# RWKV-7 layer with an int8 feed-forward on one core: the solve step's product as 64x64 matmuls over pairs of heads

## Chip, cores and metric

One core of one Trainium2 chip runs the whole program. The metric is the device time of one execution in microseconds (us), lower is better. A measurement of this kernel is the median of several runs.

## What is computed

The input x is 2 sequences of 4096 tokens with 512 channels, in float32. The layer norm of x feeds an RWKV-7 time mixing block with 16 heads of 32 channels; its result is added to x, and a second layer norm feeds a linear layer on values rounded to int8, which is added again.

```python
def step(s, inp):
    q_, w_, k_, v_, a_, b_ = inp
    sa = jnp.einsum('bhij,bhj->bhi', s, a_)
    s = s * w_[:, :, None, :] + sa[..., None] * b_[:, :, None, :] + v_[..., None] * k_[:, :, None, :]
    return (s, jnp.einsum('bhij,bhj->bhi', s, q_))
...
y = ((yg - mu) / jnp.sqrt(var + EPS)).reshape(Bx, Tx, C) * ln_w + ln_b
y = y + (rk * v.reshape(Bx, Tx, H, HS)).reshape(Bx, Tx, C)
return y * g @ Wo.T
...
x = x + attn(layernorm(x))
x = x + ffn(layernorm(x))
```

The recurrence runs over 4096 tokens per head with a 32x32 state. The kernel computes it in chunks of 32 tokens: inside a chunk the products `sa` of all tokens are the solution of a triangular system, whose inverse is built by squaring, and the state is carried from chunk to chunk.

## The kernel before

A tile is 64 tokens of both sequences (128 rows), so there are 64 tiles, and a tile has two chunks (`NC = 2`). Channels lie on the 128 partitions in 4 blocks, so a block of 128 partitions holds 4 heads of 32 channels each. A system is one head, one sequence and one chunk; a tile has 64 of them, 32 to a chunk. In a tensor such as `tx` (the inverses, 128 x 16 x 32) each quarter of the partitions holds one head, and the 16 groups are 4 channel blocks x 2 sequences x 2 chunks.

Each of the five engines has a program of its own, written out by hand as a sequence of function calls in its `tile_step`; there is no scheduler, and engines meet by semaphores alone. Three tiles are in work at a time: `mix` for tile i+1 (layer norm and the mixed inputs), `project` for tile i (the large projections), `solve` for tile i-1 (the recurrence), `finish` for tile i-2 (output projection and feed-forward). So the solve stages stand between large matmuls on TensorE, which give the other engines time.

The solve of a tile runs so. TensorE forms the scores of pairs of tokens (`scores`, L1187). `power` (L1209, three times), `half_inverse` (L1217) and `inverse` (L1225) make the inverse, with VectorE adding and transposing between them; VectorE's last addition writes `tx` and raises `v_t` (`inverse` of VectorE). Then, for each of the two chunks c:

- `from_values` (L1237) and `from_state` (L1244) sum right-hand sides, outputs and new state in PSUM; VectorE transposes the right-hand sides into `rhs_sb` (L896, `right_hand_sides`) and raises `v_rhs`
- `solve_step` (L1253) multiplies inverse and right-hand sides, and raises `p_u`
- ScalarE writes the solutions twice into `u2`, scaled by `parity[:, 0]` and by `parity[:, 1]` (`solution`, with `by_parity`), and raises `a_u`. `parity` is 1 on the partitions of the even heads and 0 on the others in its first column, and the other way round in its second, so a pair of heads in `u2` is a block-diagonal 64x64 matrix
- `from_solutions` (L1263) multiplies `u2` by `first` into outputs and new state.

Chunk 0 uses the PSUM tensor `bank_b` and chunk 1 `bank_a`. On TensorE `gate_hidden` (L1070, `xm_rg,w_gate`) stands between `solve_step` and `from_solutions` of chunk 0, and `quantised` (L1282, four transposes) between those of chunk 1.

`from_values`, `from_state`, `from_solutions` and `scores` work on pairs of heads: the stationary operand is 64x64 (the block-diagonal copies `vT2`, `s_old2`, `u2`, `bt2`, `kt2`, made by parity), and there are 16 matmuls to a chunk. `solve_step`, `power`, `half_inverse` and `inverse` work on single heads: 32x32 stationary operands, 32 matmuls to a chunk in `solve_step` and 64 to a tile in each of the others. A float32 matmul is two matmul records and two weight loads in the trace, so `solve_step` of one chunk is x64 there.

`bt2`, `kt2`, `pt` and some more lie in the memory of `w_ffn_int`, the integer weights, which are used up once they are converted. The trace names all of them `w_ffn_int`. `bt2` is written by ScalarE (`removal_pairs`) at the start of a tile's solve and read by `scores_b`, and is not read after that. Activations of ScalarE all have the line L504.

Of the kernel before, what the change touches and what calls it, by code (L numbers as in the profile page):

```python
# [14 lines left out]
CHUNK = 32  # L15
# [14 lines left out]
def count(i, per_tile, k):  # L30

    return i * per_tile + k


def rwkv_ffn_kernel(nc, a, out):
# [3 lines left out]
    NC = TB // CHUNK  # L39
    G = KB * B * NC  # L40
    GS = KB * B
# [5 lines left out]
    with ExitStack() as ctx:  # L47
        def sb(name, shape, dt=F32):
            return ctx.enter_context(nc.sbuf_tensor(name, shape, dt))

        def sem(name):
            return ctx.enter_context(nc.semaphore(name))
# [68 lines left out]
        def in_spare(groups):  # L121
# [7 lines left out]
        vT2 = sb("vT2", [P, G, 2, HS])  # L129
# [9 lines left out]
        pw = sb("pw", [P, G, 2, CHUNK])  # L139
        pt = in_spare(G)  # L140
        te = in_spare(G)
        bt2, kt2 = (in_spare(2 * G).rearrange("p (g h) t -> p g h t", h=2) for _ in range(2))
        tx = sb("tx", [P, G, CHUNK])
        rhs_sb = sb("rhs_sb", [P, GS, HS])
        u2 = sb("u2", [P, GS, 2, HS])
        state = [sb(f"state{n}", [P, GS, HS]) for n in range(2)]
# [46 lines left out]
         v_teT, v_t, v_rhs, v_state, v_rkv) = (  # L193
            sem(f"v_{n}") for n in
            "pl vraw vsum vT qkT rk blT klT pm km e ptT sums te t4 tx teT t rhs state rkv".split())
        a_pw, a_u, a_y, a_g, a_b2, a_k2, a_vT2 = (sem(f"a_{n}") for n in "pw u y g b2 k2 vT2".split())
        g_qk, g_qkf, g_rkv = (sem(f"g_{n}") for n in "qk qkf rkv".split())
        sold = sem("sold")

# [58 lines left out]
        def quad(h):  # L258
            return slice(HS * h, HS * h + HS)
# [242 lines left out]
        def _(act):  # L502
# [99 lines left out]
            def by_parity(out_, in_):  # L602
                run(out_[:, :, 0, :], in_, ACT.Identity, scale=parity[:, 0:1])
                return run(out_[:, :, 1, :], in_, ACT.Identity, scale=parity[:, 1:2])

            def solution(m, c):
                act.wait_ge(p_u, count(m, NC, c + 1))
                by_parity(u2, step_part(c, SOL)).then_inc(a_u, 1)
# [56 lines left out]
            def tile_step(i, mix=True, project=True, solve=True, finish=True):  # L665
                j, m, n = i + 1, i - 1, i - 2
                if solve:
                    removal_pairs(m)
                    key_pairs(m)
                if project:  # L670
                    keys(i)
                if finish:
                    squared_heads(n)
                if project:
                    ma_gate(i)
                    a_gate(i)
                    squares(i)
                    mk_gate(i)
                if solve:
                    power(m, 0)  # L680
                if finish:
                    log_variance(n)
                    inverse_deviation(n)
                if project:
                    decay_gate(i)
                if solve:
                    power(m, 1)
                if finish:
                    head_affine(n)
                if solve:  # L690
                    value_pairs(m)
                if project:
                    log_sigmoid(i)
                if mix:
                    normalised(j)
                if solve:
                    power(m, 2)
                if project:
                    values(i)
                if mix:  # L700
                    front_transposed(j)
                if project:
                    log_squares(i)
                    exp_tables()
                    key_decay(i)
                    exponentials(i)
                if mix:
                    low_rank(j)
                if project:
                    queries(i)  # L710
                if solve:
                    solution(m, 0)
                    output_gate(m)
                if project:
                    gate_hidden(i)
                if solve:
                    solution(m, 1)
                if finish:
                    quantised(n)
                if mix:  # L720
                    hidden(j, 0)
                    hidden(j, 1)
                if solve:
                    outputs(m, 0)
                    outputs(m, 1)
# [337 lines left out]
        def _(pe):  # L1063
            mm = nc.tensor.matmul
# [16 lines left out]
            def systems(groups):  # L1081
                return [(n, g, quad(h)) for n, g in groups for h in range(QH)]
# [3 lines left out]
            def head_pairs(groups):  # L1086
                return [(n, g, two_heads(h)) for n, g in groups for h in range(QH // 2)]

            def step_systems(c):

                return systems([(j, j * NC + c) for j in range(GS)])

            def step_pairs(c):

                return head_pairs([(j, j * NC + c) for j in range(GS)])

            def both(t):
                return t.rearrange("p h t -> p (h t)")
# [148 lines left out]

            def solve_step(m, c):
                bank = step_bank(c)
                pe.wait_ge(v_t, count(m, 1, 1))  # L1250
                pe.wait_ge(v_rhs, count(m, NC, c + 1))
                for j, g, q in step_systems(c):
                    ins = mm(bank[q, 4 * CHUNK * j + 3 * CHUNK:4 * CHUNK * (j + 1)], tx[q, g, :], rhs_sb[q, j, :],  # L1253
                             start=False, stop=True, skip_group_check=True)
                ins.then_inc(p_u, 1)

# [155 lines left out]
```

## Time and profile before

| | |
|---|---|
| runs | 3243.76 us median of 3 (3243.23 to 3243.87) |
| the profiled execution: its own time | 3244.0 us |
| its span, first to last instruction | 3242.2 us |
| TensorE matmul / weight load busy | 3029.1 us (93%) / 2675.6 us (83%) |
| VectorE, ScalarE, GpSimd busy | 2626.5 us (81%), 1974.8 us (61%), 1270.6 us (39%) |
| TensorE instructions | 84224 matmul records and as many weight loads |

"PE" is TensorE's matmuls and "PEld" its weight loads, which have rows of their own; DVE is VectorE, ACT ScalarE, POOL GpSimd. Ends of matmuls are modelled, so the time of a stage is best read from its start to the start of the next.

### The profile page before, as it was taken

The numbers are of one execution on the slowest core, as the hardware profiler recorded it, in microseconds if no ns is written. First come the engines' busy times: TensorE is split into PE (matmuls) and PEld (weight loads), VectorE is DVE, ScalarE is ACT, GpSimd is POOL, SyncE is SP. The second block draws the span as 40 slices with busy tenths as digits, with TensorE's granted clock in tenths as the row PEclk, the third lists the DMA queues.
The fourth block names the chain that finished last, engine by engine and source line by source line (L and its number), as shares of the span: only waits on it lengthen the run. The fifth ranks groups of instructions, "written<-read, shape, count | busy, mean of one in ns | idle before, by whom it ended". The sixth has DMA issues, their size and how long they took to land.

```text
span 3242.2 us, 182735 instructions
## 1 busy us (share of the span) xinstructions
PE 3029.1 (93%) x84224; PEld 2675.6 (83%) x84224; DVE 2626.5 (81%) x5443; ACT 1974.8 (61%) x3519; POOL 1270.6 (39%) x1161
## 2 busy tenths in 40 slices
PE   6999999999999999999999999999999999999996
PEld 5888888888888888888888888888888888888884
DVE  4788888888888888887888888887888878888875
ACT  3575675665665665755656656656567566566563
POOL 4334334334334344343344343443433434433332
PEclk9999999999999999999999999999999999999998
DMA  3000000000000000000000000000000000000000
GB/s 118 10 23 20 17 23 19 18 20 18 22 20 17 23 20 17 23 20 17 22 20 19 20 17 23 20 17 23 20 17 23 20 17 20 20 20 20 16 17 19
DMA packets 39380, 70.47 MB, mean 22 GB/s; under 512 B 9812, under 2 KB 10836, under 8 KB 38616
## 3 DMA queue, kind: packets, MB, share of 16 engines
q1 hardware_dynamic: 38616, 58.77, 6.8%
q8 instruction: 664, 10.88, 1.4%
q14 instruction: 100, 0.82, 0.1%
HBM read 41.97 MB, written 16.78 MB: 18 GB/s over the span
## 4 chain that ended last, share of the span: by engine, by line
PE 92%; issue 3%; ACT 2%; DVE 2%; POOL 0%; POOLq 0%; ACTq 0%; DVEq 0%
PE bank L1070 30%; PE bank_a L1209 12%; PE bank L1273 8%; PE bank_a L1187 4%; PE bank L1077 4%; PE bank_b L1187 4%; PE bank_b L1244 3%; PE bank_b L1237 3%; PE bank_a L1237 3%; PE bank_a L1244 3%; PE bank_a L1217 2%; PE bank_a L1225 2%; PE bank L1123 2%; PE bank_a L1263 2%; PE bank_b L1263 2%
## 5 line engine op out<-in xcount | busy, mean ns | idle before, releaser
L504 ACT ACT_TABLE_LOAD x383 | 491.4, 1283 | 19.1 <-DVE shift L761 12.2
L1070 PE MATMUL bank<-xm_rg,w_r 128*128 128x128 f32 x2048 | 285.4, 282 | 4.3 <-issue 3.5
L504 ACT ACTIVATE u<-bank_a,parity 128x256 f32<-128x256 f32 x128 | 53.7, 471 | 386.7 <-PE bank_a L1253 386.7
L1209 PE MATMUL bank_a<-pw,w_ffn_int 32*32 32x64 f32 x16384 | 264.6, 216 | 22.0 <-issue 17.2
L1273 PE MATMUL bank<-w_o,yc 128*128 128x512 f32 x512 | 268.9, 626 | 11.0 <-DVE yc L744 9.3
L1209 PEld LDWEIGHTS bank_a<-pw,w_ffn_int 32*32 32x32 f32 x16384 | 239.6, 106 | 41.7 <-issue 21.3
L1070 PEld LDWEIGHTS bank<-xm_rg,w_r 128*128 128x128 f32 x2048 | 248.9, 191 | 26.8 <-issue 15.9
L504 ACT ACTIVATE u<-bank_b,parity 128x256 f32<-128x256 f32 x128 | 53.8, 471 | 342.3 <-PE bank_b L1253 342.3
L1070 PEld LDWEIGHTS bank<-xm_k,w_k 128*128 128x128 f32 x2048 | 241.2, 194 | 12.5 <-issue 3.8
L1070 PE MATMUL bank<-xm_v,w_v 128*128 128x128 f32 x2048 | 250.2, 275 | 0.0
L1070 PE MATMUL bank<-xm_k,w_k 128*128 128x128 f32 x2048 | 241.7, 277 | 3.5 <-issue 3.5
L1070 PEld LDWEIGHTS bank<-xm_v,w_v 128*128 128x128 f32 x2048 | 239.3, 192 | 0.3
L870 DVE STREAM_TRANSPOSE w_ffn_int<-bank_a 128x512 f32<-128x512 f32 x192 | 137.3, 715 | 90.9 <-ACT pw L504 90.3
L399 POOL TENSOR_TENSOR yc<-yc,rkv 128x512 f32<-128x512 f32 x64 | 82.0, 1281 | 321.7 <-ACT yc L504 321.7
L396 POOL TENSOR_TENSOR kept<-ga,gma 128x512 f32<-128x512 f32 x64 | 81.5, 1274 | 311.6 <-ACT ga L504 311.6
L396 POOL TENSOR_TENSOR kkp<-kk,pinv 128x512 f32<-128x512 f32 x64 | 75.3, 1177 | 288.8 <-DVE kk L744 288.8
L396 POOL TENSOR_TENSOR kmod<-kraw,pinv 128x512 f32<-128x512 f32 x64 | 77.1, 1205 | 261.1 <-ACT pinv L504 261.1
L744 DVE TENSOR_TENSOR first<-bank_a,mask_b 128x1024 f32<-128x1024 f32 x64 | 78.4, 1225 | 106.7 <-PE bank_a L1187 106.7
L399 POOL TENSOR_TENSOR o_sb<-o_sb,x2b 128x512 f32<-128x512 f32 x64 | 81.5, 1274 | 199.3 <-DVE o_sb L968 199.3
L1209 PE MATMUL bank_a<-first,w_ffn_int 32*32 32x64 f32 x8192 | 135.0, 215 | 18.7 <-issue 17.7
L396 POOL TENSOR_TENSOR qkT<-qkT,faaaa_T 128x512 f32<-128x512 f32 x64 | 81.4, 1272 | 166.2 <-DVE qkT L914 166.2
L399 POOL TENSOR_TENSOR xm_wa<-xm_wa,xT 128x512 f32<-128x512 f32 x64 | 89.5, 1399 | 128.4 <-DVE xm_wa L779 128.4
(204 smaller groups left out, 8540.4 us busy)
## 6 DMA issues: line engine op xcount, KB each, us to landing
xin<-in_x SPq DMA_DIRECT2D x128, 128.0 KB, 2.7
xres<-in_x SPq DMA_DIRECT2D x128, 128.0 KB
out<-o_sb SPq DMA_DIRECT2D x128, 128.0 KB, 2.4
w_ffn_int<-in_weight_q SPq DMA_DIRECT2D x1, 2048.0 KB, 10.8
w_k<-in_Wk SPq DMA_DIRECT2D x1, 1024.0 KB
w_r<-in_Wr SPq DMA_DIRECT2D x1, 1024.0 KB
w_v<-in_Wv SPq DMA_DIRECT2D x1, 1024.0 KB
w_o<-in_Wo SPq DMA_DIRECT2D x1, 1024.0 KB, 14.2
```

Of the source, the lines that this page charges most:

```text
L396: return nc.gpsimd.tensor_tensor(out_, in0, in1, ALU.mult)
L399: return nc.gpsimd.tensor_tensor(out_, in0, in1, ALU.add)
L504: return nc.scalar.activation(out_, in_, func, **kw)
L870: V.transpose(pt, pairs(bank_a)[:, :, 0, :]).then_inc(v_ptT, 1)
L1070: ins = mm(bank[:, o * n:(o + 1) * n], weights[:, k, o * P:(o + 1) * P], x[:, k].rearrange("p b t -> p (b t)"), start=(k == 0), stop=(k == ...
L1077: ins = mm(bank[:, o * TOK:(o + 1) * TOK], weights[:, o * P:(o + 1) * P], hidden[:], start=True, stop=True)
L1187: ins = mm(bank[q, 64 * n:64 * n + 64], both(keys_[q, g]), both(aq[q, g, 0:2]), start=True, stop=True)
L1209: ins = mm(bank_a[q, 64 * n:64 * n + 64], pt[q, g, :], source[q, g, 0:2].rearrange("p j t -> p (j t)"), start=True, stop=True)
L1237: mm(bank[q, 4 * CHUNK * j:4 * CHUNK * j + 3 * CHUNK], both(vT2[q, g]), km[q, g].rearrange("p j t -> p (j t)"), start=(j % 4 == 0), stop=F ...
L1244: ins = mm(bank[q, 4 * CHUNK * j:4 * CHUNK * j + 3 * CHUNK], both(s_old2[q, j]), aq[q, g].rearrange("p j t -> p (j t)"), start=False, stop ...
L1263: ins = mm(bank[q, 4 * CHUNK * j + CHUNK:4 * CHUNK * j + 3 * CHUNK], both(u2[q, j]), first[q, g, 2:4].rearrange("p j t -> p (j t)"), start ...
L1273: ins = mm(fb[0][:], yc[:, k * TOK:(k + 1) * TOK], w_o[:, k, :], start=(k == 0), stop=(k == KB - 1))
```

## The change

`solve_step` uses 64x64 stationary operands over pairs of heads, 16 matmuls to a chunk where there were 32. For that ScalarE copies `tx` twice by parity into `tx2`, once per tile, in a new step `inverse_pairs`; `tx2` is the memory of `bt2`. `solve_step` waits for that copy (`a_tx2`) where it waited for `v_t`. The matmuls of a chunk stand where they stood, with the same moving operand `rhs_sb`, 32 columns, now over 64 partitions.

```diff
+        tx2 = bt2
...
+            def inverse_pairs(m):
+                act.wait_ge(v_t, count(m, 1, 1))
+                by_parity(tx2, tx[:]).then_inc(a_tx2, 1)
+
             def solution(m, c):
...
                 if solve:
+                    inverse_pairs(m)
                     solution(m, 0)
                     output_gate(m)
...
             def solve_step(m, c):
                 bank = step_bank(c)
-                pe.wait_ge(v_t, count(m, 1, 1))
+                pe.wait_ge(a_tx2, count(m, 1, 1))
                 pe.wait_ge(v_rhs, count(m, NC, c + 1))
-                for j, g, q in step_systems(c):
-                    ins = mm(bank[q, 4 * CHUNK * j + 3 * CHUNK:4 * CHUNK * (j + 1)], tx[q, g, :], rhs_sb[q, j, :],
+                for j, g, q in step_pairs(c):
+                    ins = mm(bank[q, 4 * CHUNK * j + 3 * CHUNK:4 * CHUNK * (j + 1)], both(tx2[q, g]), rhs_sb[q, j, :],
                              start=False, stop=True, skip_group_check=True)
                 ins.then_inc(p_u, 1)
```

TensorE's instructions around the two solve steps of a tile in the middle, before (a row here counts matmuls, not records; the shape is the output's, and `w_ffn_int` is `tx2`):

```order
L1244 MATMUL bank_b<-aq,s_old 64x96 x16
L1077 MATMUL bank<-hid_g,w_gate 128x128 x4
L1253 MATMUL bank_b<-rhs_sb,tx 32x32 x32
L1070 MATMUL bank<-xm_rg,w_gate 128x128 x4
L1263 MATMUL bank_b<-first,u 64x64 x16
L1123 MATMUL bank<-lo,w_maa 128x128 x16
L1237 MATMUL bank_a<-km,vT 64x96 x16
L1244 MATMUL bank_a<-aq,s_old 64x96 x16
L1253 MATMUL bank_a<-rhs_sb,tx 32x32 x32
L1282 MATMUL bank<-ident_bf,q_bf 128x128 x4
L1263 MATMUL bank_a<-first,u 64x64 x16
```

The same place in the changed kernel, where line numbers are 2 to 6 higher:

```order
L1246 MATMUL bank_b<-aq,s_old 64x96 x16
L1083 MATMUL bank<-hid_g,w_gate 128x128 x4
L1255 MATMUL bank_b<-rhs_sb,w_ffn_int 64x32 x16
L1076 MATMUL bank<-xm_rg,w_gate 128x128 x4
L1265 MATMUL bank_b<-first,u 64x64 x16
L1125 MATMUL bank<-lo,w_maa 128x128 x16
L1239 MATMUL bank_a<-km,vT 64x96 x16
L1246 MATMUL bank_a<-aq,s_old 64x96 x16
L1255 MATMUL bank_a<-rhs_sb,w_ffn_int 64x32 x16
L1284 MATMUL bank<-ident_bf,q_bf 128x128 x4
L1265 MATMUL bank_a<-first,u 64x64 x16
```

Nothing changes place; each solve step goes from 32 matmuls with a 32x32 output to 16 with a 64x32 output.

ScalarE in the same tile, before:

```order
L504 ACT_TABLE_LOAD
L504 ACTIVATE lo<-bank 128x128
L504 ACTIVATE r_raw<-bank 128x512
L504 ACTIVATE u<-bank_b,parity 128x8x32 x2
L504 ACTIVATE gate<-bank 128x512
```

and in the changed kernel:

```order
L505 ACT_TABLE_LOAD
L505 ACTIVATE lo<-bank 128x128
L505 ACTIVATE r_raw<-bank 128x512
L505 ACTIVATE w_ffn_int<-tx,parity 128x16x32 x2
L505 ACTIVATE u<-bank_b,parity 128x8x32 x2
L505 ACTIVATE gate<-bank 128x512
```

The two copies of `tx` stand between the copy of the queries and the solutions of chunk 0; no table load is added.

## Rows read from the trace of the kernel before

**Rows 1.** The page: TensorE's share, and the chain that ended last, by engine.

```profile
PE 3029.1 (93%) x84224; PEld 2675.6 (83%) x84224; DVE 2626.5 (81%) x5443; ACT 1974.8 (61%) x3519; POOL 1270.6 (39%) x1161
...
PE 92%; issue 3%; ACT 2%; DVE 2%; POOL 0%; POOLq 0%; ACTq 0%; DVEq 0%
```

**Rows 2.** Waits of TensorE, whole span: us in total, times, longest us.

```profile
PE bank_a L1253 <- DVE rhs_sb L896: 41.2, 64, 0.6
PE bank_a L1263 <- ACT u L504: 35.2, 64, 0.9
PE bank_a L1209 <- issue: 34.9, 46, 1.5
...
PE bank_a L1225 <- issue: 12.7, 17, 1.1
PE bank_a L1217 <- issue: 11.7, 16, 1.1
```

**Rows 3.** Timeline of PE, both solve steps of a tile: start us, us, what, xrecords.

```profile
1630.36 0.75 PE L1253 MATMUL bank_b<-rhs_sb,tx 32*32 32x32 f32 x64
1631.04 1.16 PE L1070 MATMUL bank<-xm_rg,w_gate 128*128 128x128 f32 x8
1632.13 1.15 PE L1263 MATMUL bank_b<-first,u 64*64 64x64 f32 x32
1633.21 1.17 PE L1123 MATMUL bank<-lo,w_maa 32*128 32x128 f32 x32
1634.32 1.54 PE L1237 MATMUL bank_a<-km,vT 64*64 64x96 f32 x32
1635.69 1.49 PE L1244 MATMUL bank_a<-aq,s_old 64*64 64x96 f32 x32
1637.82 0.74 PE L1253 MATMUL bank_a<-rhs_sb,tx 32*32 32x32 f32 x64 [0.64 <-DVE rhs_sb L896]
1638.56 0.40 PE L1282 MATMUL bank<-ident_bf,q_bf 128*128 128x128 bf16 x4
1639.50 1.15 PE L1263 MATMUL bank_a<-first,u 64*64 64x64 f32 x32 [0.54 <-ACT u L504]
1640.58 1.16 PE L1070 MATMUL bank<-xm_wa,w_hwa 128*128 128x128 f32 x8
```

**Rows 4.** Timeline of PE, the two last stages of the inverse and their successors.

```profile
1621.53 1.29 PE L1217 MATMUL bank_a<-pw,w_ffn_int 32*32 32x32 f32 x128
1622.75 1.98 PE L1273 MATMUL bank<-w_o,yc 128*128 128x512 f32 x4
...
1625.55 1.26 PE L1225 MATMUL bank_a<-pw,w_ffn_int 32*32 32x16 f32 x128
1626.74 1.12 PE L1273 MATMUL bank<-w_o,yc 128*128 128x512 f32 x2
```

**Rows 5.** Weight loads started in the first 0.15 us of L1253 and of L1263.

```profile
1630.35 0.25 PEld L1253 LDWEIGHTS bank_b<-rhs_sb,tx 32*32 32x32 f32 x20
...
1632.12 0.26 PEld L1263 LDWEIGHTS bank_b<-first,u 64*64 64x64 f32 x6
```

**Rows 6.** Groups of PE by form: busy us, mean ns of one record.

```profile
L1209 PE MATMUL bank_a<-pw,w_ffn_int 32*32 32x64 f32 x16384 | 264.6, 216 | 22.0 <-issue 17.2 <-DVE pw L744 4.7
...
L1253 PE MATMUL bank_b<-rhs_sb,tx 32*32 32x32 f32 x4096 | 48.5, 194 | 0.0
L1253 PE MATMUL bank_a<-rhs_sb,tx 32*32 32x32 f32 x4096 | 48.1, 193 | 41.2 <-DVE rhs_sb L896 41.2
```

**Rows 7.** Timeline of DVE: the last addition of the inverse.

```profile
1626.87 0.42 DVE L744 TENSOR_TENSOR tx<-bank_a,tx 128x256 f32<-128x256 f32 x1 [1.44 <-PE bank_a L1225]
```

**Rows 8.** Timeline of ACT around the place of the new step, and a parity copy.

```profile
1625.84 0.59 ACT L504 ACTIVATE r_raw<-bank 128x512 f32<-128x512 f32 x1
1631.15 0.84 ACT L504 ACTIVATE u<-bank_b,parity 128x256 f32<-128x256 f32 x2 [4.73 <-PE bank_b L1253]
...
1638.61 0.84 ACT L504 ACTIVATE u<-bank_a,parity 128x256 f32<-128x256 f32 x2 [5.96 <-PE bank_a L1253]
...
1645.18 1.33 ACT L504 ACTIVATE w_ffn_int<-bt,parity 128x512 f32<-128x512 f32 x2
```

**Rows 9.** The page: the queue that fetches TensorE's instructions.

```profile
q8 instruction: 664, 10.88, 1.4%
```

More of the change, by code:

```diff
@@ L195, in rwkv_ffn_kernel @@
             "pl vraw vsum vT qkT rk blT klT pm km e ptT sums te t4 tx teT t rhs state rkv".split())
-        a_pw, a_u, a_y, a_g, a_b2, a_k2, a_vT2 = (sem(f"a_{n}") for n in "pw u y g b2 k2 vT2".split())
+        a_pw, a_u, a_y, a_g, a_b2, a_k2, a_vT2, a_tx2 = (sem(f"a_{n}") for n in "pw u y g b2 k2 vT2 tx2".split())
         g_qk, g_qkf, g_rkv = (sem(f"g_{n}") for n in "qk qkf rkv".split())
@@ L1087, in head_pairs @@
                 return [(n, g, two_heads(h)) for n, g in groups for h in range(QH // 2)]
-            def step_systems(c):
-                return systems([(j, j * NC + c) for j in range(GS)])
             def step_pairs(c):
```

## The prediction

> **What bounds the kernel now.** First the page's busy shares: TensorE is busy 93% of the span, and it carries 92% of the chain that ended last; no other engine has over 2% of that chain [rows 1]. So a microsecond more or less in TensorE's own program comes through almost whole, and the question is what the new matmuls cost there. Second, the waits of TensorE, to see whether a solve step lies beside slack that could swallow something: chunk 1's solve step waits for VectorE's right-hand sides (64 times, 0.64 us each), and chunk 1's `from_solutions` waits for ScalarE's solutions (64 times, 0.55 us) [rows 2]. Neither is slack for the solve step: the first ends before it begins, and the second is a chain that starts at its end (solve step, two copies, next matmuls), so what is added to the step moves both. Chunk 0 has a stage of 1.09 us between solve step and `from_solutions`, and no wait; the whole stretch is TensorE's work end to end [rows 3].
>
> Third, the timeline of both steps. Chunk 0's solve step runs from 1630.36 to the next stage's start at 1631.04, **0.68 us** for 64 records. `from_solutions` of the same chunk runs from 1632.13 to 1633.21, **1.08 us** for 32 records. That one is what the new solve step will look like: 16 matmuls over pairs of heads with a 64x64 stationary operand, but with 64 moving columns where the new one has 32 [rows 3]. So the matter hangs on whether the 64 columns or something else sets those 1.08 us.
>
> **What sets a small matmul's time here.** Take 32x32 operands first. `half_inverse` moves 32 columns and takes 1.22 us for 128 records to the next start (1621.53 to 1622.75). `inverse` moves 16, half as many, and takes 1.19 us (1625.55 to 1626.74) [rows 4]. At 32 columns and fewer the time does not follow the columns; something that both share sets it, 9.4 ns a record. Then the weight loads at the start of a stage, before matmuls can hold them up. In the first 0.15 us, 20 loads of 32x32 begin in L1253, and 6 loads of 64x64 in L1263 [rows 5]: about 7.5 ns a load against 25 ns. Four 32x32 operands lie side by side on the array's diagonal, and only two 64x64 ones. If a load takes time by its columns, one of 64 takes twice as long and half as many run at once: a factor of 4 in the pace, near the 3.3 of these two rows. Over the whole of L1263, 1.08 us for 32 records is 34 ns, or 29 ns if about 0.15 us of start and end are taken off. Thus L1263 runs near the pace of its loads, although it moves 64 columns. With 32 columns the loads stay, and the pace with them. L1237 with 96 columns is slower, 1.37 us [rows 3]: there the columns do rule.
>
> **The change, part by part.**
>
> *Chunk 0's solve step.* The upper bound of the likely cost is L1263 itself, 1.08 us. Its last matmul ends sooner with 32 columns: a record of 64 columns lasts 216 ns, one of 32 lasts 193 ns [rows 6], so 1.06 us. That is 1.06 - 0.68 = **+0.38 us**. The lower end of the likely cost takes the loads at the pace of their first 0.15 us, 25 ns x 32 = 0.80 us, plus 0.15 us for start and end: 0.95 us, +0.27. I take +0.38, since the whole stage is a nearer row than its first sixth.
>
> *Chunk 1's solve step.* Here what counts is the end of its last matmul, which lets ScalarE start. The stage's duration is 0.74 us now, and that of L1263 at the same place is 1.15 us [rows 3]; less 0.03 for the shorter last record, 1.12. **+0.38 us** again. The four transposes L1282 behind it fill the wait for ScalarE and cost nothing before or after (0.40 us under 0.94).
>
> *Far bounds of both.* Below: if the pace follows columns alone, the difference of L1237 and L1263 (1.37 against 1.08 us for 32 columns more [rows 3]) puts 32 columns at 0.79 us less the 0.02, +0.09; half of L1263's 0.93 us plus 0.15 is 0.62, -0.06; and if it follows the count of instructions at the pace of 32x32, 32 x 9.4 ns + 0.15 = 0.45 us, -0.23. Above: if a pair's next load could not run beside its matmul, loads and columns add: 0.80 + 0.29 (the price of 32 columns just above) + 0.15 = 1.24 us, +0.56.
>
> *The parity copies of tx.* Two activations 128x512; the same pair on `bt` takes 1.33 us [rows 8]. VectorE finishes `tx` at 1627.29 [rows 7]; ScalarE is free since 1626.43 and next works at 1631.15 [rows 8]. So the copies run from about 1627.35 to 1628.7, and TensorE asks for them at 1630.36 [rows 3]: 1.6 us to spare. Behind the new wait on ScalarE's queue stand the solutions, which can't start before the solve step anyhow. Cost 0; without that cover it would be up to 1.4 us per tile. `tx2` uses the memory of `bt2`, whose last reader, `scores_b`, stands before the whole inverse, so it adds no wait. The copies use the same kind of activation as the solutions, and there is no table load more.
>
> *Fewer instructions.* 4096 records of matmul and as many loads go, 4.9% of TensorE's. Its stages of many short records stall on "issue" at times, 34.9 + 12.7 + 11.7 us [rows 2], and its instructions are fetched in 664 transfers [rows 9]. Those stages are untouched; the fetches only shift against them. I take -2 us, with -10 and +8 as ends, chosen from the size of these rows, which sum to 59 us: 4.9% of it is 3, and about a sixth of it either way is for the shift.
>
> *What the other engines do.* VectorE, ScalarE and GpSimd get 0.38 us more per step for the same work, so none comes onto the path; and where TensorE waits for the right-hand sides of chunk 1, that chain starts at `from_state` [rows 3], which moves along.
>
> *Sum.* 64 tiles x (0.38 + 0.38) = 48.6 us, less 2: **+47 us**. The profiled execution took 3244.0 us for a span of 3242.2, which is within 0.3 us of the median of 3243.76. So 3244 + 47 = **3291 us**, slower by 1.4%.
>
> **A rule that speaks for the change.** The rows say that a record costs by its stationary columns. The Trainium skill, page "TensorEngine Tiling (Array Packing)", section "Instruction Overhead", says that each matmul has an overhead of some 60 cycles and that one with a single free column takes as long as one with 60. By that rule half as many matmuls cost about half. The sum would be -36 us instead of +47. Rows 4 agree that few columns bring nothing, but rows 5 show that a load of a 64x64 operand is no cheaper for that.
>
> **The rivals.**
>
> *The count rules (faster).* If each matmul costs a fixed time whatever its stationary operand, 64 records at 8.8 ns (0.56 us of the 0.68) become 32, and each step drops by 0.28 us: 128 x 0.28 = 36 us, **3208 us**. It decides if 32 records need less than the present 0.56 us, under 17 ns each. For it: 16 and 32 columns cost the same. Against it: 25 ns between loads in L1263. 6%.
>
> *The columns rule (no change).* If 64x64 matmuls scale with moving columns down to 32, a step changes by -0.06 to +0.09 us (above), 128 of them by -8 to +12 us, and the time stays near **3244 us**. For it: 96 columns cost more than 64 [rows 3]. Against it: 16 cost no less than 32 [rows 4]. 5%.
>
> *Loads and matmuls do not overlap (slower still).* The Trainium skill, page "TensorE: Matmul & The Clock Gate", section "Part 3: Packing small matmuls — row/col tiling", says that a weight load overlaps running matmuls only in other rows of the array. By that rule a pair's load would wait for that pair's matmul; the trace disagrees at 64 columns, where 29 ns a record leaves no room for both. Worked out from rows, +0.56 us a step is 128 x 0.56 = 72 us, **3314 us**. 3%.
>
> *The copies come late.* If ScalarE reached them late in every tile, 1.3 us more per tile, 3291 + 83 = **3374 us**. It needs the 1.6 us to spare to vanish. 2%.
>
> **How the numbers follow.** The forecast has 84%. Its own range is 3276 (128 x 0.27 = 35 us, and up to 2 us less) to 3303 (+0.40 a step, +51, and +8 from fetches), which I take to hold 19 in 20 of it, so 80% in all; the range needs to reach no further. About 0.2%, 6.5 us, is what a measurement can tell. Slower: 84 + 3 + 2 = 89%; same 5%; faster 6%.
>
> **What would show it.** Right: the new solve step has 32 records and takes 1.0 to 1.1 us to the next start in both chunks, with loads some 27 ns apart; ScalarE's copies of `tx` end over 1 us before; TensorE waits for the solutions 0.5 us as before; a tile's period is longer by 0.76 us. Wrong: a solve step under 0.7 us, TensorE waiting for the copies of `tx`, or "issue" waits that move by over 10 us.

## The result and the profile after

| | before | changed kernel |
|---|---|---|
| median of 4 runs each | 3243.49 us (3233.72 to 3243.87) | 3303.35 us (3300.31 to 3311.68) |
| ratio, 95% interval | | 1.0199 [1.0184, 1.0213] |
| profiled execution, its time / span | 3244.0 / 3242.2 us | 3300.31 / 3298.5 us |
| mean granted TensorE clock | 0.992 | 0.985 |

The kernel is slower by about 60 us in the medians (56.3 between the two spans), where 47 was forecast. The time lies 0.35 us above the range. The sign and the main cause were right; 9 to 13 us are missing from the sum, and the experiments are mostly about them.

The page of the changed kernel: busy shares, the fetch queue, the chain by engine.

```profile
PE 3083.1 (93%) x80128; PEld 2735.6 (83%) x80128; DVE 2624.0 (80%) x5443; ACT 2059.5 (62%) x3647; POOL 1270.9 (39%) x1161
...
q8 instruction: 632, 10.35, 1.3%
...
PE 92%; issue 3%; ACT 2%; DVE 2%; SPq 1%; DMA 0%; POOL 0%; POOLq 0%; ACTq 0%; DVEq 0%
```

Against [rows 1, 9]: 4096 matmul records fewer, and yet 54 us more of busy TensorE; ScalarE 85 us more (64 x 1.33), on no chain; 32 fetches fewer.

Waits of TensorE over the whole span (us in total, times, longest us), which answer to [rows 2]:

```profile
PE bank_a L1255 <- DVE rhs_sb L902: 41.2, 64, 0.6
PE bank_a L1265 <- ACT u L505: 38.8, 64, 0.9
PE bank_a L1211 <- issue: 30.1, 42, 1.7
PE bank_a L1219 <- issue: 16.1, 17, 1.5
...
PE bank_a L1227 <- issue: 13.5, 17, 1.4
```

The wait for the right-hand sides is unchanged, the one for the solutions is 0.61 us for 0.55. There is no wait for the copies of `tx`. "issue" is idle time in which the profile shows nothing that TensorE waited for. All of TensorE's rows on it together, the small ones not shown here included, are 78.3 us before and 75.2 us after.

Timeline of PE, both solve steps of an undisturbed tile, which answers to [rows 3]:

```profile
1663.79 1.12 PE L1255 MATMUL bank_b<-rhs_sb,w_ffn_int 64*64 64x32 f32 x32
1664.85 1.16 PE L1076 MATMUL bank<-xm_rg,w_gate 128*128 128x128 f32 x8
1665.95 1.15 PE L1265 MATMUL bank_b<-first,u 64*64 64x64 f32 x32
...
1671.63 1.12 PE L1255 MATMUL bank_a<-rhs_sb,w_ffn_int 64*64 64x32 f32 x32 [0.64 <-DVE rhs_sb L902]
1672.68 0.40 PE L1284 MATMUL bank<-ident_bf,q_bf 128*128 128x128 bf16 x4
1673.68 1.15 PE L1265 MATMUL bank_a<-first,u 64*64 64x64 f32 x32 [0.60 <-ACT u L505]
```

Chunk 0's step takes 1.06 us to the next start for 0.68. In chunk 1 it is 2.05 us from the start of the step to `from_solutions` for 1.68 [rows 3], since the solutions start later by what the step grew. That is 0.38 + 0.37 = 0.75 us a tile; the shortest period of any tile goes from 47.55 to 48.29 us, 0.74 more. 64 x 0.74 = **47.4 us**.

Timelines of the weight loads at the start of chunk 0's step (cut after 0.15 us), of VectorE's last addition and of ScalarE's copies, which answer to [rows 5, 7, 8]; each is from its own engine's answer:

```profile
1663.79 0.25 PEld L1255 LDWEIGHTS bank_b<-rhs_sb,w_ffn_int 64*64 64x64 f32 x6
```

```profile
1659.89 0.42 DVE L750 TENSOR_TENSOR tx<-bank_a,tx 128x256 f32<-128x256 f32 x1 [1.75 <-PE bank_a L1227]
```

```profile
1660.35 1.33 ACT L505 ACTIVATE w_ffn_int<-tx,parity 128x512 f32<-128x512 f32 x2 [0.90 <-DVE tx L750]
```

Again 6 loads of 64x64 begin where 20 of 32x32 did. The copies end at 1661.68, 2.1 us before TensorE asks for them.

**Where the rest lies.** The mean granted clock is lower. In the middle of the run, away from start and end, the clock falls to half (1.2 GHz for 2.4) 4 times before and 15 times after; the falls in the first 115 us and the last 70 us, where the pipeline of tiles fills and drains, are left out of every count here. One such place of the changed kernel, as windows (us, busy time and count of PE, PEld, DVE, ACT, POOL, PEclk, DMA share, GB/s):

```profile
558.40:561.80 3.40, 2.15 (x54) 1.78 (x52) 3.22 (x13) 1.03 (x3) 0.86 (x2) 1.00 0.00 0
561.80:565.20 3.40, 3.40 (x40) 3.28 (x39) 3.40 (x10) 0.29 (x1) 3.06 (x3) 0.50 0.02 5
565.20:568.60 3.40, 3.40 (x28) 3.01 (x28) 3.40 (x6) 2.80 (x8) 0.51 (x2) 1.00 0.00 0
1670.42:1673.82 3.40, 2.16 (x54) 1.78 (x52) 3.22 (x13) 1.03 (x3) 0.85 (x2) 1.00 0.00 0
```

and PE's timeline there:

```profile
559.61 1.12 PE L1255 MATMUL bank_a<-rhs_sb,w_ffn_int 64*64 64x32 f32 x32 [0.65 <-DVE rhs_sb L902]
560.66 0.40 PE L1284 MATMUL bank<-ident_bf,q_bf 128*128 128x128 bf16 x4
561.66 1.87 PE L1265 MATMUL bank_a<-first,u 64*64 64x64 f32 x32 [0.60 <-ACT u L505]
563.46 1.99 PE L1076 MATMUL bank<-xm_wa,w_hwa 128*128 128x128 f32 x8
```

At half clock `from_solutions` takes 1.80 us to the next start instead of 1.08, and the next stage 1.82 instead of 0.99: 1.5 us lost. Of the 15 places in the changed kernel, 13 begin 2.1 to 2.8 us after the start of chunk 1's solve step; of the 4 before, one does. So the change adds 12 of them at one spot: right behind the new solve step, where TensorE has waited 0.65 us, worked through small matmuls, and waited 0.60 us again. The last window row, from another tile at the same point, has the same busy times, and the clock stayed up there: the busy time of a window does not tell which tiles are hit.

In the kernel before, three of the four places come behind an "issue" stall in the inverse instead. Windows and timeline of one:

```profile
1474.90:1478.30 3.40, 2.31 (x134) 1.88 (x134) 0.34 (x1) 0.87 (x2) 0.00 (x0) 0.99 0.03 7
1478.30:1481.70 3.40, 3.40 (x30) 2.26 (x30) 1.40 (x3) 0.00 (x0) 1.89 (x2) 0.50 0.03 7
```

```profile
1477.46 0.44 PE L1225 MATMUL bank_a<-pw,w_ffn_int 32*32 32x16 f32 x31 [1.09 <-issue]
1477.83 1.68 PE L1273 MATMUL bank<-w_o,yc 128*128 128x512 f32 x2
1479.44 2.60 PE L1244 MATMUL bank_b<-aq,s_old 64*64 64x96 f32 x32
```

### The profile page after: what moved, and what is told of

The parts are those of the page before. It is cut to its first block, busy times and chain, and to the rows that moved or that the text cites. A ratio compares the mean times of both kernels' runs of the same rounds, so it can differ in the third digit from the quotient of the medians.

```text
span 3298.5 us, 174671 instructions
## 1 busy us (share of the span) xinstructions
PE 3083.1 (93%) x80128; PEld 2735.6 (83%) x80128; DVE 2624.0 (80%) x5443; ACT 2059.5 (62%) x3647; POOL 1270.9 (39%) x1161
## 4 chain that ended last, share of the span: by engine, by line
PE 92%; issue 3%; ACT 2%; DVE 2%; SPq 1%; DMA 0%; POOL 0%; POOLq 0%; ACTq 0%; DVEq 0%
PE bank L1076 30%; PE bank_a L1211 12%; PE bank L1275 8%; PE bank_a L1189 4%; PE bank L1083 4%; PE bank_b L1189 4%; PE bank_b L1246 3%; PE bank_b L1239 3%; PE bank_a L1239 3%; PE bank_a L1246 3%; PE bank_a L1265 2%; PE bank_a L1219 2%; PE bank_a L1227 2%; PE bank_a L1255 2%; PE bank_b L1265 2%
## 5 line engine op out<-in xcount | busy, mean ns | idle before, releaser
L505 ACT ACT_TABLE_LOAD x383 | 491.4, 1283 | 19.0 <-DVE shift L767 12.2
L1211 PEld LDWEIGHTS bank_a<-pw,w_ffn_int 32*32 32x32 f32 x16384 | 237.1, 105 | 37.8 <-issue 17.6
L397 POOL TENSOR_TENSOR kkp<-kk,pinv 128x512 f32<-128x512 f32 x64 | 75.2, 1176 | 291.5 <-DVE kk L750 291.5
L1211 PE MATMUL bank_a<-first,w_ffn_int 32*32 32x64 f32 x8192 | 133.7, 215 | 17.7 <-issue 16.6
```

What stands on the lines that cost most here:

```text
L397: return nc.gpsimd.tensor_tensor(out_, in0, in1, ALU.mult)
L505: return nc.scalar.activation(out_, in_, func, **kw)
L1211: ins = mm(bank_a[q, 64 * n:64 * n + 64], pt[q, g, :], source[q, g, 0:2].rearrange("p j t -> p (j t)"), start=True, stop=True)
```

## The experiments

The kernel before ran beside each set; its median there was 3226.7 to 3237.0 us, so ratios compare better than times. e1 to e4 ran on one chip, e5 to e8 on a second, e9 to e12 on a third, e13 to e15 on a fourth, e16 and e17 on a fifth. "Stretches" counts the falls to half clock in the middle of the profiled execution. e11 and e14 are one kernel, and their profiled spans differ by 11 us (3192.8 and 3204.3).

| kernel | median, us | ratio to before [95%] | clock | stretches |
|---|---|---|---|---|
| e1_copies | 3230.64 | 1.0004 [0.999, 1.0018] | 0.992 | 2 |
| e2_cols16 | 3304.79 | 1.0224 [1.0201, 1.0246] | 0.985 | 18 |
| e3_even_heads | 3220.48 | 0.9965 [0.9954, 0.9976] | 0.992 | 1 |
| e4_lock_good | 3477.12 | 1.0781 [1.0725, 1.0838] | 0.966 | 55 |
| e5_after_again | 3297.28 | 1.0212 [1.0185, 1.0239] | 0.983 | 19 |
| e6_align_good | 3239.74 | 1.0033 [1.002, 1.0046] | 0.981 | 24 |
| e7_align_bad | 3423.57 | 1.0595 [1.0573, 1.0618] | 0.984 | 18 |
| e8_only_chunk0 | 3247.27 | 1.004 [1.0014, 1.0066] | 0.994 | 0 |
| e9_only_chunk1 | 3279.09 | 1.0133 [1.0099, 1.0166] | 0.985 | 15 |
| e10_split_u | 3226.88 | 0.9981 [0.9971, 0.9992] | 0.993 | 0 |
| e11_fill | 3196.24 | 0.9888 [0.9871, 0.9904] | 0.994 | 1 |
| e12_fill_split | 3202.33 | 0.9901 [0.9886, 0.9916] | 0.993 | 0 |
| e13_tiny_fill | 3232.95 | 0.9979 [0.9966, 0.9992] | 0.979 | 24 |
| e14_fill_again | 3198.37 | 0.9874 [0.9854, 0.9894] | 0.992 | 0 |
| e15_waits_again | 3241.79 | 1.0013 [1.0001, 1.0025] | 0.981 | 20 |
| e16_before_fill13 | 3185.3 | 0.9873 [0.9856, 0.989] | 0.992 | 0 |
| e17_before_fill25 | 3227.2 | 1.0002 [0.9991, 1.0013] | 0.994 | 0 |

### The parts of the change: e1, e2, e3

e1: the kernel before, with the new step `inverse_pairs` on ScalarE and nobody who reads it.

```diff
+            def inverse_pairs(m):
+                act.wait_ge(v_t, count(m, 1, 1))
+                by_parity(tx2, tx[:]).then_inc(a_tx2, 1)
...
+                    inverse_pairs(m)
```

> The kernel before plus the two parity copies of tx on ScalarE and nothing else: the solve step keeps its 32x32 matmuls on tx and its wait for v_t; the copies are read by nobody. My theory (the copies lie in a stretch in which ScalarE is idle): 3243 us, within 7 us of the kernel before, ScalarE busy some 85 us more. Rival (the copies delay the solutions, or a part of the 60 us is theirs): over 3255 us.

1.0004 [0.999, 1.0018]: the copies cost nothing, and ScalarE is busy 84.7 us more, as expected.

e2: the changed kernel, with 16 moving columns where it has 32.

```diff
-                    ins = mm(bank[q, 4 * CHUNK * j + 3 * CHUNK:4 * CHUNK * (j + 1)], both(tx2[q, g]), rhs_sb[q, j, :],
-                             start=False, stop=True, skip_group_check=True)
+                    ins = mm(bank[q, 4 * CHUNK * j + 3 * CHUNK:4 * CHUNK * j + 3 * CHUNK + HALF], both(tx2[q, g]),
+                             rhs_sb[q, j, 0:HALF], start=False, stop=True, skip_group_check=True)
```

> The changed kernel with 16 instead of 32 moving columns in each solve-step matmul, so the other half of the solutions is left out; stationary operands, count and order are as in the changed kernel. Theory (weight loads of 64 columns set the pace): the solve step of chunk 0 stays at 1.04 to 1.05 us to the next start and the time at 3300 us within 8. Rival (moving columns set it): some 0.2 us less per step, 25 us in all, 3277 us.

e3: the changed kernel, with the even heads' 32 stationary columns alone.

```diff
-                    ins = mm(bank[q, 4 * CHUNK * j + 3 * CHUNK:4 * CHUNK * (j + 1)], both(tx2[q, g]), rhs_sb[q, j, :],
-                             start=False, stop=True, skip_group_check=True)
+                    even = slice(q.start, q.start + HS)
+                    ins = mm(bank[even, 4 * CHUNK * j + 3 * CHUNK:4 * CHUNK * (j + 1)], tx2[q, g, 0, :],
+                             rhs_sb[q, j, :], start=False, stop=True, skip_group_check=True)
```

> The changed kernel with 64x32 stationary operands: only the columns of the even head of each pair are loaded and multiplied, the solutions of the odd heads are left out. 16 matmuls per chunk and 32 moving columns as in the changed kernel, half the stationary columns. Theory (stationary columns set the pace): loads 27 ns instead of 53 per pair of records, the solve step falls to 0.55 to 0.70 us and the time by some 45 to 60 us to 3240 to 3256. Rival (64 rows, or something that goes with the pairs, set it): the step stays over 0.95 us and the time near 3300.

PE's timeline at chunk 0's step, of e2 and then of e3:

```profile
1652.64 1.11 PE L1255 MATMUL bank_b<-rhs_sb,w_ffn_int 64*64 64x16 f32 x32
1653.68 1.16 PE L1076 MATMUL bank<-xm_rg,w_gate 128*128 128x128 f32 x8
```

```profile
1668.76 0.69 PE L1256 MATMUL bank_b<-rhs_sb,w_ffn_int 64*32 64x32 f32 x32
1669.39 1.16 PE L1076 MATMUL bank<-xm_rg,w_gate 128*128 128x128 f32 x8
```

Half the moving columns: 1.04 us for 1.06, next to nothing. Half the stationary columns, with the same 32 records: 0.63 us. The step is set by the columns of its stationary operands, as the prediction had it; whether loading them or multiplying with them takes the time, the two runs do not tell apart. e3 came 20 us under its expectation. It has one stretch at half clock and is 84 us faster than e2, which ran beside it, while its two steps are shorter than e2's by only some 0.83 us a tile, 53 us. Of the other 31 us, 17 stretches fewer would give 20 at 1.2 us each and 27 at 1.6, and the "issue" waits 4 (70.6 for 74.2 us).

### One chunk at a time: e8, e9

e8 has the 64x64 step in chunk 0 alone, e9 in chunk 1 alone. The edit of e9 (in e8 `c == 0`):

```diff
-                for j, g, q in step_pairs(c):
-                    ins = mm(bank[q, 4 * CHUNK * j + 3 * CHUNK:4 * CHUNK * (j + 1)], both(tx2[q, g]), rhs_sb[q, j, :],
+                for j, g, q in step_pairs(c) if c == 1 else step_systems(c):
+                    inv = both(tx2[q, g]) if c == 1 else tx[q, g, :]
+                    ins = mm(bank[q, 4 * CHUNK * j + 3 * CHUNK:4 * CHUNK * (j + 1)], inv, rhs_sb[q, j, :],
```

> The changed kernel with the 64x64 matmuls in chunk 0 only; chunk 1 has its 32x32 matmuls on tx again. Theory: chunk 0's step 1.05 us and chunk 1's 0.74 as before, so half of the price, 24 us over the kernel before, with stalls at block boundaries free to move it by 10: 1.0045 to 1.0110 times the time before.

> The changed kernel with the 64x64 matmuls in chunk 1 only; chunk 0 has its 32x32 matmuls again. Block stalls apart, this should equal the run with chunk 0 only (24 us over the kernel before). New theory, from the granted clock of the traces so far: the changed kernel has some 15 stretches of 3.4 us at half the clock in the middle of its span, the kernel before 4, the run with chunk 0 only none; they begin at chunk 1's solve step, which lies between two waits, and where the array has half as much to do per us when its matmuls are 64x64. It expects 10 or more such stretches here and 35 to 45 us over the kernel before, clearly more than chunk 0 alone. Rival (the extra is block stalls alone): 18 to 30 us over it, and under 5 such stretches.

Chunk 0 alone costs 16 us, chunk 1 alone 44, though the step grows by the same 0.37 us in both (24 us each). e8 lies just below its expectation of 1.0045, e9 within its own. e8 has no stretch at half clock, e9 has 15, and 12 of them begin 2.0 to 2.8 us after chunk 1's solve step starts. In chunk 0 large matmuls follow the step at once; in chunk 1 four transposes and a wait do.

e10 took the other side: the kernel before, with ScalarE handing over the solutions in two halves, so that TensorE waits 0.33 us instead of 0.55 for them.

```diff
-                by_parity(u2, step_part(c, SOL)).then_inc(a_u, 1)
+                for half in (slice(0, GS // 2), slice(GS // 2, GS)):
+                    by_parity(u2[:, half], step_part(c, SOL)[:, half]).then_inc(a_u, 1)
```

> The kernel before with one edit: ScalarE copies the solutions in two halves of the pairs and TensorE's from_solutions starts after the first half. Every tile waits 0.55 us for these copies in chunk 1, on the chain. Theory: the wait falls by 0.35 to 0.4 us, 23 us less in all, given back in part by block stalls: 0.990 to 0.997 times the time before. Rival (the wait's time comes back at the next one): no change.

0.9981 [0.9971, 0.9992]: 64 x 0.22 would be 14 us, and 8 came in the medians; both are less than expected. A shorter wait there gains little, and the kernel before has few falls of the clock to lose.

### The ends of the instruction blocks: e4, e5, e6, e7

The stalls on "issue" do not fall anywhere. Of the 94 us by which the tiles of the kernel before exceed their shortest form in jumps of over 150 ns, 93.5 us sit where TensorE's instruction count stands at the same place of a block of 256 (the count modulo 256). The queue that fetches instructions moves 10.88 MB in 664 transfers [rows 9], 16.4 KB each. The Trainium skill, page "Runtime: NRT & Kernel Launch", section "Instruction fetch mechanics", gives blocks of 256 instructions and calls the cost of passing from one to the next mostly hidden. The block size agrees with the trace. "Mostly hidden" agrees by count alone: 112 "issue" waits stand against the 664 transfers, but they take 78.3 us, up to 3.5 us each, and in e7 below 202 waits against 640 transfers take 182.7 us. A tile has 2656 instructions on TensorE before and 2528 after, 10.375 and 9.875 blocks, so the ends wander through the tile in both. With 2560 they stay where they are, and a few small matmuls at the start of the program choose where.

e5 is the changed kernel again, beside e6 to e8. e4 brings the changed kernel to 2560 by 32 instructions of satisfied waits in one place. Such an instruction waits for a semaphore that has long had its value, and two `wait_ge` make one instruction:

```diff
+            def pad(n):
+                for _ in range(2 * n):
+                    pe.wait_ge(const_done, 1)
...
+                    pad(32)
...
+            pad(240)
```

> The changed kernel unaltered, so that the others of this set have it on the same chip. Theory: slower than the kernel before by 1.5 to 2.2%, of which 47 us are the two solve steps.

> The changed kernel with waits added on TensorE that are always satisfied: enough for 32 more instructions per tile, so that a tile is 2560 instructions, ten blocks of 256, and enough ahead of the first tile to put the first solve step of chunk 1 at place 59 in its block of 256. The work is the same. Theory (the 9 us that the forecast missed, and about 115 us of the changed kernel in all, are stalls at the boundaries of fetched blocks of 256 instructions, and only where two boundaries lie close together in time): every tile has the same stalls, few ones at this place, 48.9 to 49.3 us per tile and 3220 to 3250 us in all, faster than the changed kernel by over 50 us although it has more instructions. Rival (stalls on issue come from the number of instructions or from chance): 3300 us or more.

e5 came as expected: 1.0212, 66 us in the medians, with 19 stretches. e4 lost some 180 us against it instead of gaining. Waits of TensorE in e4:

```profile
PE bank_a L1243 <- issue: 169.5, 64, 2.8
...
PE bank L1110 <- issue: 36.5, 1, 36.5
...
PE bank_a L1215 <- issue: 3.3, 10, 1.0
```

The stalls in the inverse did go (3.3 us), but the 32 instructions of satisfied waits cost 2.6 us a tile where they stand (169.5 / 64), about 83 ns each, a price that my expectation had left out. The 240 at the start cost some 20 us once: TensorE's first matmul begins at 36.5 us, and at 14.6 in the changed kernel. The clock fell too, in 55 places, and 36 of these begin during the 32 waits of a tile or right behind them.

e6 and e7 spread the waits over four places between large matmuls (8 instructions each, `pad(8)`), and differ from each other by one number:

```diff
-            for _ in range(41):
+            for _ in range(7):
                 mm(fb[0][0:HS, 0:HS], ident[0:HS, 0:HS], ident[0:HS, 0:HS], start=True, stop=True)
```

> The changed kernel with the satisfied waits that fill a tile to 2560 instructions spread over four places behind large matmuls (8 instructions each), where the sequencer is ahead of the array, and with 41 small matmuls at the very start, under the wait for x, that set the place of the first block boundary. In the trace of the locked version tried before, the issue waits of the dense stages had gone (3 us where there were 60) and the 32 instructions in one place cost 2.7 us per tile in themselves. Theory (stalls come where the boundaries of blocks of 256 instructions fall): the boundaries fall at a good place in every tile, issue waits under 15 us in all, 48.4 to 48.9 us per tile, 3190 to 3230 us in all. Rival (the added waits cost their time wherever they stand): over 3400.

> The same program with 7 instead of 41 small matmuls at the start: nothing else differs, and every boundary of a block lies 136 instructions later in the tile. Theory: 1.5 to 3.5 us more stall in every tile than with 41, 3300 to 3420 us. Rival (the place of the boundaries does not matter): the same time as with 41, within 10 us.

Waits of TensorE in e6, and in e7:

```profile
PE bank_a L1215 <- issue: 7.4, 21, 0.6
```

```profile
PE bank_a L1215 <- issue: 113.5, 125, 1.7
PE bank L1279 <- issue: 55.6, 62, 2.3
```

41 against 7 small matmuls before the loop: 3240 against 3424 us, 184 us for nothing but the place of the block ends. All "issue" waits of TensorE sum to 12.2 us in e6 and 182.7 in e7. In the change itself, where the ends wander before and after, the shift was worth 3 us.

e6 came 10 us above its expectation, e7 4 us above. Against the changed kernel in e5, which ran beside it, e6 has 66 us less of "issue" waits (12.2 for 78.0) and is 58 us faster, and its clock stays as low, with 24 stretches for 19. So the block ends are one matter and the clock another, and e6 has mended only the first.

### The clock by itself: e11 to e15

e11 fills the two waits of chunk 1 with matmuls of no use, 6 before the solve step and 10 before `from_solutions`, which bring a tile to 2560 instructions without any wait instruction:

```diff
+            def fill(i, n):
+                for _ in range(n):
+                    mm(bank_b[:, 0:HS], ident_bf[:], ident_bf[:, 0:HS], start=True, stop=True)
...
+                if solve and mix:
+                    fill(j, 6)
...
+                if solve and mix:
+                    fill(j, 10)
...
+            for _ in range(57):
+                mm(fb[0][0:HS, 0:HS], ident[0:HS, 0:HS], ident[0:HS, 0:HS], start=True, stop=True)
```

> The changed kernel at 2560 instructions per tile again, with the block boundaries at the place that was good, but the filling is now 16 bf16 matmuls of 32 moving columns into a part of PSUM that nobody reads any more: 6 ahead of chunk 1's solve step and 10 ahead of its from_solutions, in the two waits of 0.6 us. Against the run with the good place and waits as filling (3240 us, clock 0.981): theory (the half clock comes from the array being too idle around chunk 1) under 6 stretches at half clock in the middle, clock over 0.989, 10 to 20 us less, 3220 to 3230. Rival (idle time there does not bring the half clock): clock stays at 0.981 and the time at 3240.

e12 has 8 and 4 such matmuls, 8 instructions of waits, and the split solutions of e10.

> The same with ScalarE's copies of the solutions in two halves and the filling changed to 8 and 4 matmuls and 4 instructions of waits. Theory: another 20 to 25 us off, 3195 to 3210 us, faster than both kernels by over 0.5%.

e11 comes to 3196 us, 1.1% under the kernel before and well under its expectation, with the 64x64 steps still in it. e12 lies in its range, but it was to take another 20 to 25 us off, and it is 6 us slower than e11. But e11 differs from e6 in three things: the filling, the place of the block ends, and the missing waits. So e13 keeps every instruction of e11 where it is and makes the filling tiny:

```diff
-                    mm(bank_b[:, 0:HS], ident_bf[:], ident_bf[:, 0:HS], start=True, stop=True)
+                    mm(bank_b[0:HS, 0:1], ident_bf[0:HS, 0:HS], ident_bf[0:HS, 0:1], start=True, stop=True)
```

> The kernel of e11_fill with every instruction in its place, only the 16 filling matmuls of a tile made tiny: a 32x32 stationary operand and 1 moving column in place of 128x128 and 32 columns. If the gain of e11_fill over e6_align_good (3196 against 3240 us) is the clock, held up by what the filling does on the array, the tiny filling loses it: 15 or more half-clock stretches in the middle of the run, a granted clock of 0.980 to 0.988, and 3225 to 3245 us. If it is the place of the block ends, or the time that the filling takes on the queue, nothing changes: clock 0.993 to 0.994 and 3190 to 3200 us.

> e11_fill again on the chip of e13_tiny_fill, as the base of that comparison: 3190 to 3200 us and clock 0.994 by every theory.

> e6_align_good again on the same chip: 3230 to 3250 us and clock 0.98 by every theory; should it come near e11_fill here, the 44 us between them were no property of the two kernels.

PE's timeline at chunk 1's step in e13, at one of its half-clock places:

```profile
1236.34 0.30 PE L1108 MATMUL bank_b<-ident_bf 32*32 32x1 bf16 x6
1237.06 1.12 PE L1263 MATMUL bank_a<-rhs_sb,w_ffn_int 64*64 64x32 f32 x32 [0.42 <-DVE rhs_sb L902]
1238.11 0.40 PE L1292 MATMUL bank<-ident_bf,q_bf 128*128 128x128 bf16 x4
1238.44 0.40 PE L1108 MATMUL bank_b<-ident_bf 32*32 32x1 bf16 x10
1239.11 1.73 PE L1273 MATMUL bank_a<-first,u 64*64 64x64 f32 x32 [0.28 <-ACT u L505]
1240.77 2.07 PE L1076 MATMUL bank<-xm_wa,w_hwa 128*128 128x128 f32 x8
```

and in e14:

```profile
1228.63 0.31 PE L1108 MATMUL bank_b<-ident_bf 128*128 128x32 bf16 x6
1229.35 1.12 PE L1263 MATMUL bank_a<-rhs_sb,w_ffn_int 64*64 64x32 f32 x32 [0.40 <-DVE rhs_sb L902]
1230.40 0.40 PE L1292 MATMUL bank<-ident_bf,q_bf 128*128 128x128 bf16 x4
1230.63 0.40 PE L1108 MATMUL bank_b<-ident_bf 128*128 128x32 bf16 x10
1231.40 1.15 PE L1273 MATMUL bank_a<-first,u 64*64 64x64 f32 x32 [0.36 <-ACT u L505]
```

Everything is alike but the work inside the filling. The windows of 3.40 us up to each of these places differ hardly in busy time, e13 and then e14:

```profile
1236.00:1239.40 3.40, 2.71 (x73) 2.29 (x70) 3.23 (x12) 1.19 (x3) 0.85 (x2) 1.00 0.00 0
```

```profile
1228.14:1231.54 3.40, 2.64 (x70) 2.31 (x68) 3.22 (x13) 1.04 (x3) 0.86 (x2) 1.00 0.00 0
```

e13 has 24 stretches, e14 none. The "issue" waits sum to 17.7 and 17.6 us. The spans are 3241.9 and 3204.3 us: 37.6 / 24 = **1.6 us a stretch**, near the 1.5 us read off the timeline; the medians, 34.6 us apart, give 1.4. So of the 43 us between e15 and e14 (e6 and e11 again, on this chip) 35 come from what the filling does on the array, and the clock goes with them; neither the place of the blocks nor the time that the filling takes differs between e13 and e14. The other 9 us, between e15 and e13, are not the clock's, for e15 has the fewer stretches (20 for 24); they belong to the waits or to the place of the blocks, which no run tells apart. e13, e14 and e15 took the times that were expected.

### The same treatment for the kernel before: e16, e17

The kernel before with the same filling (2688 instructions a tile, 10.5 blocks, so that only every second tile has the block ends in one place), and 13 or 25 small matmuls at the start.

> The kernel before with the 16 filling matmuls per tile of e11_fill and 13 small matmuls at the start: 2688 instructions to a tile, 10.5 blocks, so that every second tile meets the block ends in the same places (43 and 171 where chunk 1's solve step starts). By the account so far its solve steps are 47 us cheaper than those of e11_fill and its stalls at block ends about 1.3 us a tile against 0.3, since only every second tile can be placed well: 3200 - 47 + 65 = 3218 us, 3195 to 3230, with a clock of 0.993. If the 64x64 step were what makes e11_fill fast, this kernel would stay at 3230 to 3245 us.

> The same with 25 small matmuls at the start: places 91 and 219 in place of 43 and 171. The model of the fetches gives this place about 0.1 us a tile more than e16: within 15 us of it, clock 0.993.

e16 is the fastest kernel of the study at 3185 us, ratio 0.9873 [0.9856, 0.989], 10 us under its expectation; e17, 12 small matmuls later, gains nothing, and missed its expectation by 27 us. The sums of "issue" are 42.1 and 76.6 us, which is 35 of the 42 us between them. By the spans e16 lies where the account puts it: in it the solve steps are 47.4 us cheaper and the "issue" waits 24.5 us dearer than in e14 (42.1 against 17.6), 23 us in all, and the spans differ by 21 us (3183.3 against 3204.3). But e14 and e16 ran on different chips, where the kernel before itself took 3236.96 and 3226.68 us; by the ratios, 0.9874 and 0.9873, the gap between e14 and e16 is nearer zero than 21. Which of the two is right stays open, since they never ran side by side. What e16 does show is that the gain of e11 does not need the 64x64 step.

## Why the prediction was right and where it failed

**TensorE is the bound; the solve step's cost comes through whole.** Right. The chain is 92% TensorE again, and both waits of chunk 1 moved along.

**The stationary columns set the pace.** Right. Chunk 0 went by +0.38 us as forecast, chunk 1 by +0.37 for +0.38. e2 and e3 rule the other readings out: going down to 16 moving columns does next to nothing, and half the stationary columns give 0.63 us.

**Parity copies at nothing.** Right, by e1 and by the rows: 2.1 us to spare where 1.6 was forecast.

**Fewer instructions, -2 us, -10 to +8.** The size was right (78.3 to 75.2 us), the reason was poor. It is no matter of a few per cent fewer instructions but of where the ends of the fetched blocks fall, and e6 and e7 lie 184 us apart on that alone. Here they wander through all stages before and after, and so the sum hardly moved.

**The rivals.** *The count rules*: 32 records would have had to take under 0.56 us; they take 1.06. The Trainium skill's figure of some 60 cycles a matmul (page "TensorEngine Tiling (Array Packing)", section "Instruction Overhead") does not price this step; its stationary columns do. *The columns rule*: excluded by e2. *Loads and matmuls do not overlap*: by that rival the step would take 1.24 us, and it takes 1.06; and half the moving columns would have taken 0.14 us off in e2, where 0.02 came. The rule that the prediction cites does not ask for 1.24 us, though: consecutive pairs stand in different halves of the array's rows (`two_heads(h)` alternates), so this says nothing against the rule. The time came near that rival's 3314 us, but not by its mechanism. *The copies come late*: excluded by e1.

**The step that failed: the sum has no term for TensorE's clock.** It priced what stands in the queue and took the clock as given; the half-clock row at 1478 us was in the trace of before, with 1.09 us of idle ahead of it, and was not looked at. The change lets the clock fall in 15 places for 4. At 1.2 us (tiles of the changed kernel with a stretch last 51.1 us in the mean, those without 49.9) to 1.6 us (e13 against e14), 11 more are 13 to 17 us. A third reading agrees: over the 85 runs of the kernel before that stand beside the experiments, each compared with the others on its chip, the time is longer by 2.4 us for each 0.001 that the granted clock is lower, which makes 17 us from 0.992 to 0.985. The account of the two profiled executions is then:

| | us |
|---|---|
| two solve steps, 64 x 0.741 | +47.4 |
| "issue" waits, 78.3 to 75.2 | -3 |
| 11 more stretches at half clock | +13 to +17 |
| sum | +57 to +61 |
| measured, spans | +56.3 |

The medians, at 60, lie in it. In e5 they are 66 us apart, with 19 stretches. The range missed by only 0.35 us because its upper end had 8 us for fetches and 2 for longer steps; neither came, so that nearness is luck.

**What stays open.** What decides in which tiles the clock falls: windows with the same busy times stand ahead of a fall and of none. e13 and e14 show that the work done on the array matters and not how long TensorE is busy, but no run varied it in steps. And e8 cost 16 us where its step alone would be 24; it had none of the four falls of before, which would be 5 to 6 us, and its "issue" waits are 71.1 us for 78.3; together these are more than the 8, within an interval of 8 us either way.

## What to carry to other kernels

Price a small matmul by the columns of its stationary operand: merging two 32x32 blocks into one block-diagonal 64x64 halves the instructions and leaves twice the columns to each with half as many blocks side by side, and here it cost 0.37 us a step. Read the granted clock of the stretches around the place that a change touches, above all where waits and small matmuls alternate, and give it a term of its own in the sum. Before judging a change of a per cent or two in a long unrolled program, look whether the stalls on "issue" moved; here the place of block ends alone was worth up to 184 us, and large-operand matmuls in idle gaps were worth 35 (e13 against e14).

## What the runs showed of the hardware that was not expected

- The clock fell to half without a long idle: behind two waits of 0.65 and 0.60 us with 32 matmul records of 64x64 stationary operands and four transposes between them, in 13 tiles of 64. With 16 matmuls of 128x128 and 32 columns in those gaps it did not fall in the middle of the run (e14), with 16 of 32x32 and one column it fell 24 times (e13).
- An instruction of satisfied waits on TensorE is not free: some 83 ns each where 32 stand together (2.6 us a tile in e4).
- The stalls on "issue" repeat at one place of TensorE's instruction count modulo 256 (93.5 of 94 us), and between two choices of where that place falls in the tile lie 184 us of 3240 (e6 and e7).
- Two 32x32 operands replaced by one 64x32 operand take 0.63 us for 32 records, against 0.68 us for 64 records of 32x32 [rows 3]. Half as many records save nearly nothing: one of 64x32 comes every 20 ns where one of 32x32 came every 11, with two side by side in place of four.
